# A selective-scan block on one core: ScalarE's exponentials queued one place earlier, and VectorE's two row blocks moved to the second and sixth place

## What is computed

```python
proj = hidden_states @ in_proj_w            # x and z
xc = silu(conv4(x))                         # 1024 channels
dt = softplus(dt_r @ dt_proj_w + dt_bias)   # Bm, Cm: rows of 16, normalised
def step(h, inp):
    x_t, dt_t, B_t, C_t = inp
    dA = jnp.exp(dt_t[..., None] * A)
    dBx = dt_t[..., None] * B_t[:, None, :] * x_t[..., None]
    h = dA * h + dBx
    y = jnp.einsum('bdn,bn->bd', h, C_t)
    return (h, y)
s = ((ys + D * xc) * silu(z)) @ out_proj_w.T
g = silu(ffn(xn))                           # gate, up (1376 wide), down; dequantised, with low rank parts
out = x + s * g
```

## The kernel before

| quarter | VectorE | ScalarE | TensorE |
|---|---|---|---|
| 0 | S0, hidden | exp for S0, copies of tb 2, 3 | turns 2, 3 |
| 1 | S1, sum of tb 0 | exp for S1, copy of tb 4 | turns 0, 4 |
| 2 | S2 | exp for S2, tanh, copies of tb 5, 6 | turns 5, 6 |
| 3 | S3, silu, sum of tb 1 | exp for S3, copy of tb 7 | turns 1, 7 |

## Time and profile before

### The profile page before, as it was taken

How to read it: one execution, slowest core, us unless ns; L and a number is a source line. 1 busy time by engine, 2 the same in 40 slices (tenths; PEclk the granted TensorE clock), 3 DMA queues, 4 the chain that set the end, 5 groups by cost and what they waited for, 6 DMA issues and landing times.

```text
span 1402.8 us, 13293 instructions
## 1 busy us (share of the span) xinstructions
PE 1200.2 (86%) x4598; PEld 658.4 (47%) x4598; DVE 1036.0 (74%) x827; ACT 732.9 (52%) x892; POOL 762.7 (54%) x418
## 2 busy tenths in 40 slices
PE   4999828889988688999999982888998778899998
PEld 3664415445543344555444541454554334455543
DVE  2866478989948989997425537989984899899740
ACT  2111566667638566774012266666763856677400
POOL 1000048889923688895130005888982378889511
PEclk9779879999998899999999986999999989999999
DMA  6542114989961188898811111588986118889860
GB/s 210 202 138 85 41 58 106 219 197 218 232 160 60 60 211 205 196 226 195 311 39 38 45 46 51 126 208 206 223 214 156 60 60 216 207 194 223 195 231 37
DMA packets 60612, 214.08 MB, mean 153 GB/s; under 512 B 6362, under 2 KB 6490, under 8 KB 60132
## 3 DMA queue, kind: packets, MB, share of 16 engines
q0 software_dynamic: 16128, 88.09, 32.2%
q1 hardware_dynamic: 42836, 119.50, 24.6%
q10 hardware_dynamic: 1584, 5.68, 1.0%
HBM read 102.18 MB, written 22.98 MB: 89 GB/s over the span
## 4 chain that ended last, share of the span: by engine, by line
PE 30%; POOL 27%; DVE 18%; DMA 9%; issue 8%; ACT 6%; SPq 1%; POOLq 0%; DVEq 0%; ACTq 0%
POOL ub L529 25%; DVE hb L1103 10%; PE psA L747 9%; PE psM L947 7%; DMA bn<-ss_rows_scratch 4%; PE psM L773 3%; DVE th L972 2%; DMA dt<-w_out_dram 2%; PE psM L794 2%; PE psT L870 2%; POOL yT L540 2%; DMA yT<-yc 2%; PE psA L843 1%; DVE hb L972 1%; DVE yT L972 1%
## 5 line engine op out<-in xcount | busy, mean ns | idle before, releaser
L529 POOL TENSOR_TENSOR ub<-dtx,bn 128x1024 f32<-128x1024 f32 x256 | 625.1, 2456 | 115.4 <-DVE hb L1103 101.3
L1103 DVE TENSOR_TENSOR_SCAN hb<-psA,ub 128x1024 f32<-128x1024 f32 x256 | 584.7, 2285 | 70.9 <-ACT psA L646 64.2
L870 PE MATMUL psT<-ident,hb 128*128 128x128 f32 x2048 | 275.1, 277 | 135.0 <-DVE yT L972 76.0
L870 PEld LDWEIGHTS psT<-ident,hb 128*128 128x128 f32 x2048 | 232.4, 142 | 302.0 <-issue 125.6
L773 PE MATMUL psM<-xnT,w_ts 128*126 128x512 f32 x704 | 345.1, 622 | 30.0 <-DVE hid L972 22.1
L665 ACT ACTIVATE yc<-psT,ssm 128x512 f32<-128x512 f32 x336 | 219.0, 685 | 214.6 <-PE psT L870 214.4
L646 ACT ACTIVATE psA<-dt,cc 128x1024 f32<-128x1024 f32 x256 | 285.6, 1116 | 35.5 <-DVE hb L1103 35.5
L522 POOL TENSOR_TENSOR dtx<-dt,xc 128x1024 f32<-128x1024 f32 x12 | 28.2, 2353 | 362.1 <-DVE dt L1087 362.1
L773 PEld LDWEIGHTS psM<-xnT,w_ts 128*126 128x126 f32 x704 | 128.5, 199 | 148.6 <-issue 123.0
L892 PE MATMUL psM<-w_dn,hid 126*128 126x512 f32 x352 | 165.0, 597 | 0.0
L972 DVE SCALAR_TENSOR_TENSOR yT<-psT,ssm,yT 128x512 f32<-128x512 f32 x144 | 104.9, 735 | 33.2 <-DMA yT<-yc 31.9
(11 more groups left out here) (88 smaller groups left out, 807.7 us busy)
## 6 DMA issues: line engine op xcount, KB each, us to landing
yT<-yc POOLq DMA_DIRECT2D x112, 768.0 KB, 6.5
bn<-ss_rows_scratch SPq DMA_DIRECT2D x64, 512.0 KB, 4.9
w_ts<-w_gu_scratch SPq DMA_DIRECT2D x44, 504.0 KB, 3.4
w_ts<-w_in_dram SPq DMA_DIRECT2D x32, 256.0 KB, 3.5
z_scratch<-th SPq DMA_DIRECT2D x32, 256.0 KB, 5.8
hb<-z_scratch SPq DMA_DIRECT2D x16, 512.0 KB, 9.1
w_gu_scratch<-hid ACTq DMA_DIRECT2D x11, 504.0 KB, 3.2
yT<-x_dram SPq DMA_DIRECT2D x2, 2048.0 KB, 12.5
```

The source lines that it names most:

```text
L529: pool.tensor_tensor(ub[:, i % 2, :], dtx[:, i, :], bn[:, t, :], ALU.mult).then_inc(s_u, 1)
L870: mm = pe.transpose(psT[:, at % 2, i * P:(i + 1) * P], hb[:, t * DH + i, tb * P:(tb + 1) * P], ident[:, :])
L1103: dve.tensor_tensor_scan(hb[:, t * DH + i, :], psA[:, i % 2, :], ub[:, i % 2, :], 0.0, ALU.mult, ALU.add).then_inc(s_scan, 1)
```

## The change

In `decay`'s calls the exponential of the next unit is issued where that of the current one was, with one extra call ahead of the loop, and the last quarters have one call less. `Y_ORDER` puts tb 0 and 1, VectorE's blocks, at the second and sixth place instead of the third and seventh; the other six keep their order. In `slot`, `silu_gate` stands behind the loop over sums, which in the last quarter is now empty.

```diff
-Y_ORDER = [2, 3, 0, 4, 5, 6, 1, 7]
+Y_ORDER = [2, 0, 3, 4, 5, 1, 6, 7]
@@ scalar
+                    decay(1, 0)
                     for n in range(LATE):
                         for i in range(DH):
-                            decay(n + 1, i)
+                            decay(n + 1 + (i + 1) // DH, (i + 1) % DH)
                             if i == 2:
                                 tanh_gate(n + FILL, (n + FILL) % 2)
                             for tb in Y_ORDER[2 * i:2 * i + 2]:
                                 if not by_dve(n, tb):
                                     scale_y(n, tb)
                     for p in range(QUARTERS):
-                        if p + 4 < QUARTERS:
-                            decay(LATE + 1 + p // 4, p % 4)
+                        if p + 5 < QUARTERS:
+                            decay(LATE + 1 + (p + 1) // 4, (p + 1) % 4)
@@ vector, def slot(n)
                             scan(n + 1, 1 - n % 2, i)
-                            if i == DH - 1:
-                                silu_gate(n + FILL, (n + FILL) % 2)
                             for tb in Y_ORDER[2 * i:2 * i + 2]:
                                 if by_dve(n, tb):
                                     add_y(n, tb)
+                            if i == DH - 1:
+                                silu_gate(n + FILL, (n + FILL) % 2)
```

## The result

The changed kernel takes 1368.25 us in the median of four runs (1362.66 to 1369.48), the kernel before 1402.43 (1399.99 to 1403.41) beside it: a ratio of 0.9749 (95% interval 0.9733 to 0.9766), 34 us less. The forecast was 1361, so it comes 7 us later, inside the range of 1350 to 1385. The profiled execution took 1369.48 us with a span of 1367.7, against 1404.62 and 1402.8: 35.1 less.

The account below looks back on a forecast made before the run. Bound by a loop of VectorE's sum, transposes, copies, exponential and scan. Gains of 31.9 (steady slots), 3.3 (first slots) and 6.0 us (late quarters) sum to 41.2, taking the median from 1401.92 to 1361 us; range 1350 to 1385.

Parts of the forecast that it names:

- The loop and the exponential: Steady slots: VectorE's sum, transposes, copies, exponential and scan form a loop; both idle pieces, 1.20 us a slot, go.
- Steady slots, 31.9: Seven steady slots in each of four halves: from 12.64 to 11.50 us each, 31.9 us gained, bounds 26.3 and 33.6.
- GpSimd's product for the next S0: Steady slots: the product for the next slot's first scan, behind the gather's issue, ends at 11.48 us, wanted at 11.44.
- First slots, 3.3: First slot of each half: half of the 6.6 us left of exponential waits, 3.3 us gained, bounds 0 and 6.6.
- Late slots, 6.0: Late quarters with z and down-projection steps: 1.5 us gained a half, 6.0 in all, bounds -4 and 14.4.
- bound of 14.4 from TensorE's waits: Late quarters: TensorE waits only 3.6 us a half ahead of transposes, so at most 14.4 us can be gained.
- rival A: Steady and late slots: transfers become the bound; 1390 us, or mildly 1372; chance 0.22, mostly the mild form.
- spare of 4.2 us between issue and need: B-row loads: 9.1 us from free buffer to need, 4.2 beyond the 4.9 us median landing; said against the transfer bound.
- Between the halves and at the end nothing moves.: Before scans, between halves and at the end: zero gain; state 14's gather and what follows move with the last copy.
- B (slower): Chain through ScalarE from scan end to sum is longer than laid out, 2.4 us to spare; 1432 us; chance 0.03.
- C: Exponentials can't start earlier, waiting for the scan two units before, and the second part fails too; 1402 us; chance 0.03.
- D: TensorE's late-quarter idle time goes nearly whole and first slots give all; 52.2 us gained, 1350 us; chance 0.10.

Follow-up runs that it names:

- e7_short: Changed kernel with GpSimd's product over 896 of the 1024 time steps, part of the scan's input left out; 1362.28 us, one run.
- e1_order: Kernel before with only `Y_ORDER` changed (row blocks at the second and sixth place), exponentials left where they were; 1370.15 us, ratio 0.9757.
- e4_bload: Changed kernel with SyncE's loads of B rows 11 and 14 issued ahead of a z store and two gate-weight loads; 1358.44 us, ratio 0.9679.
- e5_both: Exponentials one place ahead, row blocks left at the third and seventh place, and loads of B rows 11 and 14 issued earlier; 1347.65 us, ratio 0.9608.
- e6_before_b: Kernel before with only the loads of B rows 11 and 14 put earlier in SyncE's order; 1400.04 us, ratio 0.9996.
- e3_back: Changed kernel with the four z-row loads at a half's end held back until the last gather has landed; 1369.01 us, ratio 0.9746.
- e2_ahead: Changed kernel with the old block order and silu place, so only the exponentials go one place ahead; 1361.01 us, ratio 0.9696.
- e8_tail: e5_both with z rows issued behind the next half's small loads in the first half of each sequence; 1346.06 us, ratio 0.9606.

## Why the prediction was right, and where it was not

- *The loop and the exponential.* Right. The idle time of scans from the exponential fell from 64.2 to 1.9, and it reappears as waits of the exponentials for scans (171.1 us). The runs add what the prediction had left open: either of the two parts takes the steady slots to 11.5 by itself.
- *Steady slots, 31.9.* Right: 33.0, slots of 11.46 against 11.50. The step that named GpSimd's product for the next S0 as what is late next is confirmed by the rows of the slot and by e7_short. One price in it was off: VectorE's own time is 11.24, not 11.44. The prediction took the two idle pieces away from 12.64 and kept the rest. But an idle piece is counted from the full end of the instruction before, and an instruction that need not wait starts a little before that end: S2 to S3 was 2.28 + 0.86 us, and two scans without a wait are 4.38 for both (269.44 to 273.82), 2.19 each. With some 0.1 at each of the two places the slot is 11.24. Thus GpSimd's lateness is worth 0.22 a slot, 6 us in all, where the prediction had made it 0.06. The 11.48 of its chain came out although two of its terms were off: the product behind the gather's issue took 2.69 us and not 2.36, but began 0.61 after the issue's start and not 0.88.
- *First slots, 3.3.* Mis-sized, measured 5.7 of at most 6.6: nearly nothing took the exponential's place there. e1_order, in which the exponentials stay where they were, gains only 2.4 there.
- *Late slots, 6.0.* Measured 2.3. With the B rows out of the way e4_bload gains 11.5 here over before, within the bound of 14.4 from TensorE's waits. e5_both gains 15.7: the bound left out the waits for B rows, and their order alone is worth 3.9 in the kernel before (e6_before_b). What failed is the pricing of rival A. It was weighed as a bound of bandwidth, with all stages paying, and dismissed by a spare of 4.2 us between issue and need; but that sum let the row be issued as soon as its buffer is free, whereas in late slots SyncE issues row 11 behind a store that waits for data and row 14 behind two loads of weights, and they then land in 8.1 to 14.0 us where these slots are long, not in 4.9. The prediction had the 13.29 us and the 2.44 of idle time in view and took them for the state of the DMA engines. The order of the queue costs 9.2 us there (339.9 to 330.7).
- *Rival A.* As a bound of bandwidth it did not come: the steady slots run at a DMA share of 1.00 in single slots (0.95 predicted) and 0.89 over all seven, and still take 11.46. The landing times grew, of B rows from 4.9 to 6.1 us and of gathers from 6.5 to 7.1 in the median, within what was to spare. The growth agrees with the Trainium skill, "DMA: Bandwidth & Descriptors", section "Issuing engines are not separate DMA queues": transfers of all issuing engines interleave on the same 16 engines. The plainest case of it here is e3_back, where GpSimd's last gathers land in 5.7 to 5.8 us without SyncE's loads beside them and in 11.4 to 12.4 with them. Rival A's late rows were real in the late slots, in the mild form, and in three steady slots of e2_ahead.
- *"Between the halves and at the end nothing moves."* Wrong by 7.4 us, a term of zero. The step took the gather's landing as a constant that moves with its issue, and TensorE's durations behind it as fixed. At the last end it lands 0.9 later, and the longer standstill then costs TensorE's clock, another 1.1; at the third end the gather is no later, and the end is longer by 1.5 with the lower clock. e3_back shows that the loads of z rows hold the gather, but also that holding them back moves the wait to what stands behind them. What makes the landing later than before, and how much of the 7.4 us each cause has, stays open.
- *The sum.* It is closer than its terms: first slots gave 2.4 more than forecast, steady slots 1.1, and the work ahead of the scans, where nothing was changed, was 1.5 shorter in the profiled execution. That is luck, and it hides near half of what late slots (3.7) and ends (7.4) fell short by.
- *Range and rivals.* B (slower) had 2.4 us to spare in its chain, and nothing of it was seen. C fell: the copies had held the exponential. D (1350, with a late gain of 12) was in reach for the late slots, 11.5 in e4_bload, but took another edit.

The signs that were named: slots of 11.5 (11.46), scans idle for GpSimd's products (13.3 us), transposes at a slot's start free of the sum, and the late stretch at 82.4 (83.66, which is where the reader should have looked for B rows).

## What to carry over

When an in-order engine produces for the bound engine and also serves others, issue its product one place ahead; then look for how many instructions stand between the two consumers that free the next producer's buffer, since a second fix of the same loop can cost instead of adding (0.22 us a slot here). Read the order of the DMA queue for each load that a shorter stage will want earlier: what may be issued early has to stand ahead of every store that waits for data, and such a loss can be too small to measure before the change and worth over a quarter of its gain after (9.8 of 34 us). Before a load is moved behind others, look for what stands behind its new place and who waits for that: both edits at the ends of halves made a new wait of the one they took away. The end of a stage is a term of its own, never a zero, when transfers of the stage are still landing in it.

## What the runs showed of the hardware

- A slot whose 16 DMA engines are busy 1.00 of the time isn't necessarily bound by them: with 0.86 in a slot of 12.64 us and 1.00 in one of 11.45, the engines were busy for 10.9 and 11.4 us, while the slot's length was set by GpSimd. In e4_bload the late stretch got shorter at a share that rose from 0.94 to 0.97.
- A product of GpSimd right behind the issue of a gather is recorded longer: 2.97 and 2.69 us in the slot above, 2.35 for the one that isn't; over all 104 of them the median is 2.67. One issue in ten took 1.19 us or more, the median was 0.89. Over all products the mean rose from 2456 to 2580 ns when the slots became shorter, so an engine's price read from a loose schedule was 5% too low in the tight one.
- TensorE kept its full clock after a standstill of 1.77 us (and eight transposes took 1.31) and came out of one of 3.76 at the lower clock (1.97 for eight transposes). The wait grew by 2.0 us, of which 0.9 was a later landing and the rest work done sooner; with the clock the end was 1.9 us longer. At the third end a standstill of 1.78 left the clock at 1.00 and one of 2.01 was followed by the lower one.
- A gather of 768 KB landed in 5.7 to 5.8 us with four loads of 512 KB issued behind its landing (e3_back), and in 11.4 to 12.4 us with them beside it (after); 256 KB stores took 2.0 us alone and 5.6 to 6.4 right behind four such loads (e5_both, e8_tail).
